# Feed forward work queued between the last attention heads in place of a barrier

## What is computed

```python
x = x + _L1_xattn_ref(_layernorm(x, axis=-1), ctx_2048, itok_BxS_0_1023, ...)
x = x + _L1_ffn_ref(_layernorm(x, axis=-1), ...)
```

```python
h = jax.nn.gelu(jnp.einsum('lne,he->lnh', x, proj1) + proj1_bias, approximate=False)
out = jnp.einsum('lnh,eh->lne', h, proj2) + proj2_bias
```

## Time and profile before

| | us |
|---|---|
| median of 3 executions | 3270.91 (3270.78 to 3271.13) |
| profiled execution | 3268.49 |
| span of its profile | 3266.7 |
| PE busy in the span | 3162.6 (97%) |
| DVE busy | 2159.1 (66%) |
| ACT busy | 1261.4 (39%) |
| POOL busy | 1126.1 (34%) |

### The profile page before, as it was taken

The page is one execution under the profiler, slowest core; times in us unless marked ns, Lnnn a source line. Parts: engine busy times, 40 slices in busy tenths (PEclk is TensorE's granted clock), DMA queues, the critical chain, the costliest instruction groups (busy, mean ns, idle before and its releaser), DMA issues.

```text
span 3266.7 us, 51561 instructions
## 1 busy us (share of the span) xinstructions
PE 3162.6 (97%) x18517; PEld 2687.2 (82%) x18517; DVE 2159.1 (66%) x5741; ACT 1261.4 (39%) x3041; POOL 1126.1 (34%) x1179
## 2 busy tenths in 40 slices
PE   7999999999999789999999999999998999999999
PEld 4666666689899579999999999999997888888887
DVE  6888888755555568877788888877776533333332
ACT  2333333333444345555555555555554311111111
POOL 6877777535344322222222222222201011000110
PEclk9999999999999899999999999999999999999999
DMA  4544443269677721111111111111101300000000
GB/s 127 151 142 140 132 133 103 81 198 328 214 234 225 242 72 53 46 46 46 46 46 46 45 38 42 46 46 46 34 14 55 98 26 26 26 26 26 26 14 14
DMA packets 129418, 285.92 MB, mean 88 GB/s; under 512 B 18840, under 2 KB 19488, under 8 KB 129168
## 3 DMA queue, kind: packets, MB, share of 16 engines
q1 hardware_dynamic: 100080, 186.49, 18.3%
q0 software_dynamic: 29088, 96.13, 8.9%
HBM read 177.98 MB, written 104.58 MB: 86 GB/s over the span
## 4 chain that ended last, share of the span: by engine, by line
PE 79%; DVE 9%; POOL 7%; DMA 2%; ACT 1%; issue 1%; SPq 0%; POOLq 0%; DVEq 0%
PE g_PH L1021 11%; PE g_O L1044 11%; PE t_U L1486 10%; PE t_S L1438 9%; PE t_PO L1473 5%; PE t_M L1422 5%; PE t_T L1460 3%; POOL c_kf L355 3%; PE f_Y L664 2%; PE f_Y L893 2%; PE t_M L1377 2%; PE f_Y L387 2%; PE f_Y L382 2%; DVE c_R L400 2%; DVE c_z L394 2%; PE t_M L1359 2%
## 5 line engine op out<-in xcount | busy, mean ns | idle before, releaser
L1448 ACT ACTIVATE t_pr<-t_sm,t_nb 128x256 f32<-128x256 f32 x512 | 256.6, 502 | 368.2 <-DVE t_nb L1444 368.2
L1392 POOL TENSOR_TENSOR t_r<-t_r 128x256 f32<-128x256 f32 x128 | 96.1, 751 | 778.9 <-DVE t_rw L1454 451.4
L1034 DVE CAST g_hh<-g_hf 128x512 fp32r<-128x512 f32 x128 | 61.8, 482 | 435.7 <-PE g_O L1044 427.0
L355 POOL TENSOR_TENSOR c_kf<-c_vt,c_ct 128x512 f32<-128x512 f32 x256 | 297.0, 1181 | 0.0
L1033 ACT ACTIVATE g_hf<-g_PH,g_b1s 128x512 f32<-128x512 f32 x128 | 88.2, 689 | 519.1 <-PE g_PH L1021 518.3
L1455 DVE TENSOR_SCALAR t_pr<-t_pr,t_rw 128x256 f32<-128x256 f32 x512 | 222.0, 434 | 18.1
L387 PE MATMUL f_Y<-c_kh,c_th 128*128 128x512 f32 x448 | 200.1, 447 | 10.5 <-ACT c_kh L362 10.5
L1021 PE MATMUL g_PH<-g_xh,g_w1h 128*128 128x512 f32 x512 | 205.8, 402 | 1.5 <-DVE g_xl L1009 1.5
L1021 PE MATMUL g_PH<-g_xh,g_w1l 128*128 128x512 f32 x512 | 203.5, 397 | 0.0
L1021 PE MATMUL g_PH<-g_xl,g_w1h 128*128 128x512 f32 x512 | 203.1, 397 | 0.0
L1044 PE MATMUL g_O<-g_w2h,g_hh 128*128 128x512 f32 x512 | 202.4, 395 | 0.0
(11 more groups left out here) (345 smaller groups left out, 9706.6 us busy)
## 6 DMA issues: line engine op xcount, KB each, us to landing
xs<-c_zero SPq DMA_DIRECT2D x71, 256.0 KB, 5.2
f_xg<-xs SPq DMA_DIRECT2D x71, 256.0 KB, 3.4
ys<-f_yt POOLq DMA_DIRECT2D x71, 256.0 KB, 3.6
c_tr<-kpad SPq DMA_DIRECT2D x60, 256.0 KB, 4.7
f_xg<-xn SPq DMA_DIRECT2D x40, 256.0 KB, 4.7
c_xt<-x SPq DMA_DIRECT2D x32, 256.0 KB, 3.5
c_cr<-ctx SPq DMA_DIRECT2D x32, 256.0 KB, 4.0
c_ct<-ctxh SPq DMA_DIRECT2D x32, 256.0 KB, 4.1
```

The lines of the kernel that those rows point to most:

```text
L355: T["kv", h] = T["kv1", n] = p.do("gpsimd", lambda e: e.tensor_tensor(o, iv, ic, ALU.mult), g("vt", h), g("ct", h), g("kl", n - 8), g("kh" ...
L1448: T["ex", x] = p.do("scalar", lambda e, t=t, k4=k4: e.activation(pr[:, N % 2, t, :], sm[:, k4, :], ACT.Exp, bias=nb[:, k4, 0:1], scale=-1. ...
```

## The change

The dense phase no longer has a `Phase` of its own: it appends to the attention's lists. `ffn_phase` becomes a generator, and the attention's loop runs pieces of it after iterations N = 248 to 256. What it waits for is named per buffer.

```diff
+        if N == total - 8:
+            mem.close()
+            mem2 = ExitStack()
+            dense = ffn_phase(nc, Scope(ctx.keep, mem2), d, p, T, *small, ident, mhalf, c_id, c_mh, lambda: [T["out", batches - 1], *p.last()])
+            next(dense)
+        if total - 7 <= N <= total:
+            next(dense, None)
+    for _ in dense:
+        pass
...
+    gone = (A["ctfree", B - 1], A["pmx", 2 * B - 1], A["qcp", B - 1], A["krp", B - 1], A["krl", B - 1])
+    for i in range(4):
+        T["x0", i] = p.dma("sync", dx0[i], lambda e, i=i: e.dma_start(xts[0][:, i, :], d["x3g"][0][:, i, :]), A["out", 1], *gone)
...
+    yield
+    for i in range(2):
+        stats(i)
+        yield
+        norm(i)
+        yield
+    stats(2)
+    fetch(0, A["rs", 2 * B * NH // 4 - 1])
+    yield
+    norm(2)
+    stats(3)
+    yield
+    norm(3)
+    place_weights(0, A["vo", total - NH + 2], "gpsimd")
+    turn(0, O[0], A["pm", 0])
+    turn(1, O[1], A["pm", 1])
+    yield
+    turn(2, O[2], A["pm", 2])
+    turn(3, O[3], A["am", total - 1])
+    yield
+    over = A["vo", total - 1]
+    fetch(1)
+    T["hf", -2], T["hf", -1], T["pmfree",] = A["ptl", total - 1], A["otl", total - 1], A["add", 2 * B - 2]
+    for e_ in ("sync", "gpsimd"):
+        p.hold(e_, *end())
+    T["b2",] = p.dma("sync", db[1], lambda e: e.dma_start(b2s[:, :], d["f1b2"]))
+    load(1)
...
+                place_weights(k + 1, over)
+                if k + 2 < NB:
+                    fetch(k + 2)
```

More of the change, by code:

```diff
@@ L921, in front_phase @@
     return p
[L927 to L1103, removed]
-    total = groups * NB
-    def prepare(G, k, where):
-        for late, o in nxt.get((k, where), []):
-            H = G + 1 - late
-            if 0 < H < groups and (H < NG or o[0] in "SNT"):
-                {"S": stats, "N": norm, "T": turn}[o[0]](4 * H + int(o[1]))
-    for n in range(total + 2):
-        G, k = divmod(n, NB)
-        if n < total:
-            if G == 0 and k + 1 < NB:
-                place_weights(0, k + 1)
-                if k + 2 < NB:
-                    fetch(0, k + 2)
-            prepare(G, k, 0)
-            first(G, k)
-            prepare(G, k, 1)
-        if n >= 2:
-            G2, k2 = divmod(n - 2, NB)
-            second(G2, k2)
-            if (G2 + 1) % NG == 0 and G2 + 1 < groups:
-                if k2:
-                    place_weights(G2 + 1, k2 - 1)
-                fetch(G2 + 1, k2)
-                if k2 == NB - 1:
-                    place_weights(G2 + 1, k2)
-            if k2 in (5, 7, 9, 11):
-                raise_(G2, (k2 - 5) // 2)
-            if k2 == NB - 1:
-                for t in range(4):
-                    evac(G2, t)
-                if G2 + 2 < groups:
-                    load(G2 + 2)
-                if G2 + 1 < groups:
-                    load_acc(G2 + 1)
-        if n < total:
-            hidden(G, k)
-    return p
@@ L1147, in attention_phase @@
-def attention_phase(nc, ctx, d, front, idx, gat, ident, mhalf, batches=B):
+def attention_phase(nc, ctx, mem, d, front, idx, gat, ident, mhalf, small, batches=B):
     p = Phase(nc, ctx, "t", [])
@@ L1705, in groups @@
         return [v[g] for g in range(8)]
-    xs = {n: groups(d[n]) for n in ("x3", "out")}
+    d["x3g"], d["outg"] = groups(d["x3"]), groups(d["out"])
     with ExitStack() as keep:
@@ L1712, in program @@
         mhalf = keep.enter_context(nc.sbuf_tensor("mhalf", [128, 1], F32))[:, :]
-        makers = [
-            lambda ctx, before: front_phase(nc, ctx, d, before, d["xa"], idx, gat, ident, mhalf),
-            lambda ctx, before: attention_phase(nc, ctx, d, phases[0], idx, gat, ident, mhalf),
-            lambda ctx, before: ffn_phase(nc, ctx, d, before, "g", xs["x3"], [None], [xs["out"]], [list(range(16))], d["f1w1"], d["f1w2"],
-                                          d["f1b1"], d["f1b2"]),
-        ]
-        phases, before = [], []
-        for make in makers:
-            with ExitStack() as mem:
-                phases.append(make(Scope(keep, mem), before))
-            before = phases[-1].last()
+        small = [keep.enter_context(nc.sbuf_tensor(n, shape, F32))[tuple(slice(None) for _ in shape)]
+                 for n, shape in (("b1g", [128, 16]), ("stg_", [128, 2, 6]), ("agg", [128, 2, 2]), ("rsg", [128, 2, 1]))]
+        with ExitStack() as mem:
+            phases = [front_phase(nc, Scope(keep, mem), d, [], d["xa"], idx, gat, ident, mhalf)]
+        mem = ExitStack()
+        phases.append(attention_phase(nc, Scope(keep, mem), mem, d, phases[0], idx, gat, ident, mhalf, small))
+        before = phases[-1].last()
         with nc.Block() as block:
```

135 lines of the change are left out of this document (added).

## The result

The kernel with the change takes **3248.22 us** (median of four, 3243.99 to 3249.23), the kernel before on the same chip 3271.02: ratio 0.9924, interval 0.9911 to 0.9936 (the ratio is taken over all executions, so it is not quite the quotient of the two medians). The profiled execution is the fastest of the four: 3243.99 us, span 3242.2, that is 24.5 us less than the span before.

The account below looks back on a forecast made before the run. PE, busy in 97% of the span, was taken as the bound, so only its idle seam could give time: 12.1 - 1.5 - 0.8 = 9.8 us less, 3270.9 - 9.8 = 3261.1, range 3255.0 to 3266.0.

Parts of the forecast that it names:

- The step that failed: Dense steps after step 2's first products: they follow without a gap and stay as they are, gain 0.
- All signs that I had named: Profile after: PE goes on within 0.3 us, waits once for 6 to 8, clock falls to 0.50, heads lose 2 to 3.
- the seam: From the last attention product to the end of step 2's first products: 30.8 us becomes 18.7, 12.1 less.
- The wait at step 2: PE stands still 7.3 us for step 2's weights, queued on SP behind the output transfer, `b2s` and 1 MB.
- The clock: PE's granted clock falls again in the wait at step 2, costing 3.0 us; bounds 0 and 3.0.
- The last heads: Work moved into the attention's last heads costs PE 1.5 us for transposes and 0.8 for a stretch.
- The transposes: PE's 16 transposes in the last heads: 1.8 us, partly filling a 0.25 wait for DVE, net 1.5.
- The stretch: Last heads: one DVE piece slowed beside POOL's weight split, 0.96 less 0.2 slack, 0.8 us on PE; bounds 0 and 2.7.
- The collision: POOL's weight split, 1.27 + 1.48, runs beside the last head's scaling or the fourth `norm` on DVE and slows it.
- the one without a wait at step 2: Rival, chance 0.07: step 2's weights are there when PE wants them; 20.1 us go, giving 3250.8.
- The last heads did not give the gain back: Rival, chance 0.16: DVE's added 9.2 us delay PE; 3264.9 if half does, 3269.5 if all.
- no later step waited for weights: Rival, chance 0.03: weights no longer keep up over 13 refills after step 2; slower above 6.8 us per cycle.

Follow-up runs that it names:

- wlast_timed: Kernel before, barrier and order of work kept, with only the four dense weight tiles allocated last: 3251.85 us, ratio 0.9947.
- after_w64: Changed kernel with 64 bytes left free ahead of the dense weights, block 0 waiting for one head more: 3259.13 us, ratio 0.9972.
- after_fetch2b: Changed kernel with block 2's weights fetched ahead of SP's hold and group 1's 1 MB moved behind block 3's transfers: 3237.60 us, ratio 0.9895.
- best_front: Changed kernel with earlier weight fetches, statistics and norms, plus 96 bytes left free ahead of kh and kl in the front: 3234.31 us, ratio 0.9898.

## Why the prediction was wrong, step by step

- **The step that failed**: "From there on the steps follow without a gap, and the change leaves them as they are." Without a gap was right; "as they are" was not. The new layout made the operands' starts agree modulo 256, and each of 3072 products became some 5 ns shorter: 16.5 us in the profile, 17.2 timed alone (wlast_timed). With the old difference put back (after_w64) the change gives 9.9 us. I took PE at 100% busy and clock 1.00 for PE at its pace, and looked at the moved tiles only for what they wait for. All signs that I had named came true (PE went on after 0.23 us, stood still once, for 7.0, the clock fell, the heads lost 2.2): they were all about the seam, and none could have shown this. That after_w64 comes within 0.1 of the forecast is in part luck, as the terms below were off both ways.
- **The wait at step 2**: 7.0 us against 7.3, ended by DVE's rest of `g_w`, as said. The blocks landed at 2523.24 + 5.67 = 2528.91, 6.6 us after the output transfer (2519.14 + 3.18 = 2522.32), against 6.9.
- **The clock**: it fell to 0.50, but late in the wait, and cost 2.1 (2.7 in after_w64, where the next 12 second products lost 0.35 more) against 3.0.
- **The last heads**: 2.2 against 2.3, but from other terms. The transposes cost their full 1.76 and not 1.5, because PE still waited for DVE's `otl` behind them. The stretch cost 0.44 and not 0.8: the last 12 `vo` products start 1.47 us behind the `vo` product ahead of them (2513.49 to 2514.96) where it was 1.03 (2508.53 to 2509.56). The collision came at the fourth `norm`, beside POOL's split of block 0. Timeline of DVE after:

```profile
2510.32 1.47 DVE L1489 TENSOR_SCALAR g_xn<-g_x,agg,rsg 128x512 f32<-128x512 f32 x1
2511.70 1.27 DVE L1502 TENSOR_TENSOR g_xl<-g_O,g_xh 128x512 fp32r<-128x512 f32 x2
```

  and of POOL:

```profile
2510.21 2.72 POOL L109 TENSOR_TENSOR g_w<-g_stg,g_w 128x512 fp32r<-128x512 f32 x2 [2.19 <-ACT g_w L108]
```

  One `norm` was stretched, by 0.93 against the 0.54 of the others; the second split found DVE at `xl`, which did not slow. So there was one collision, and not one for each of POOL's two splits. The Trainium skill (SBUF — State Buffer, Who interferes with whom) says that a `tensor_scalar` can run in a mode that takes the port pair which DVE shares with GpSimd, and that whichever instruction comes second is then blocked until the first ends; one with at most one input in SBUF, outside such a mode, does not contend. The trace agrees: the `norm`, a TENSOR_SCALAR, ends at 2511.79, just behind POOL's first split (2510.21 + 1.29 = 2511.50), and the `xl`, with its other input in PSUM, keep their 0.68.
- **The rivals**: the one without a wait at step 2 was not what happened; the run that makes it so (after_fetch2b) has PE waiting 0.8 us in all. The last heads did not give the gain back, and no later step waited for weights.

## What to carry to other kernels

When a change moves tiles, read the pace of the products (their number in a window where PE is fully busy) as a term of the sum. For long runs of products like these, give the two operands starts that agree modulo 256 bytes, which costs a pad; here it paid 17.2 us in the dense phase, and nothing in the front, where PE does not set the end. Ahead of a queue's hold put whatever is needed soonest and does not need it, and put a large transfer behind the small ones that are needed first. The waits of 7.0 and 2.9 us also cost the clock behind them (4.80 and 4.5 us for 12 products); those of 0.4 in after_fetch2b, at a granted clock of 1.00, did not.

## What was not expected of the hardware

A product of 128x512 (float32 in its rounded form) follows the one before after 226.7 ns where its moving and its stationary operand start alike modulo 256 bytes in their partition, and after 231 to 233 on average where the weights start 64 or 128 bytes past the rows. Where only one weight plane in three disagrees, its own products are hit (236 against 226 to 229). The fast rhythm is very even: 12 products take 2.719 to 2.721 us in every step of the kernel after that has no transposes. The Trainium skill says that PE reads its moving operand and its weights through two independent ports (SBUF — State Buffer, Who interferes with whom). That gives no reason for the starts to matter; the runs show that they do. Why is not shown. In short runs of products among others the medians are 228 to 232 ns with starts alike, too (attention's `vo`, and the front in best_front), and products of other shapes were not tried.
